# Unit 0's key transfers and row maxima issued from ScalarE's queue, unit 1's input load moved back, and ten constant passes in place of twelve

## The reference

```python
x = x + 0.5 * ffn(layernorm(x), conv_w, conv_b, wqkv, bqkv, wo, bo, ...)   # _L0_ffn_ref
x = x + attn(layernorm(x), Wq, bq, Wk, bk, Wv, bv, Wo, bo)                 # _L0_attn_ref
x = x + 0.5 * ffn(layernorm(x), conv_w, conv_b, wqkv, bqkv, wo, bo, ...)
```

## Time and profile before

| | before |
|---|---|
| median of three executions | 1558.99 us |
| the profiled execution, device time | 1559.22 us |
| its span in the trace | 1557.5 us |
| PE busy | 1502.6 us (96%) |
| DVE, ACT, POOL busy | 1160.8, 1121.3, 1014.9 us |
| chain that ended last, by engine | PE 84%, DVE 8% |
| instructions | 26116 |

### The profile page before, as it was taken

One profiled execution on the slowest core, in us unless ns is written; L12 is line 12 of the kernel. 1 busy time (PEld: TensorE's weight loads), 2 busy tenths in 40 slices (PEclk: granted clock), 3 DMA queues, 4 the chain that ended last, 5 costly groups with the idle time before them and its releaser, 6 DMA issues.

```text
span 1557.5 us, 26116 instructions
## 1 busy us (share of the span) xinstructions
PE 1502.6 (96%) x8318; PEld 832.5 (53%) x8318; DVE 1160.8 (75%) x1834; ACT 1121.3 (72%) x1636; POOL 1014.9 (65%) x978
## 2 busy tenths in 40 slices
PE   4888999999999999999999999999999999999997
PEld 3433555555555555555555555555555555555476
DVE  3767677878778787777877778777777777767486
ACT  2466777677776777777677777777777777777776
POOL 3521668767686776868767686776757677667343
PEclk7799999999999999999999999999999999999999
DMA  7433333152332514233142331514323251521111
GB/s 177 119 92 86 96 87 85 49 140 53 81 91 56 130 42 105 74 88 91 49 131 61 81 92 45 141 48 116 83 75 98 69 117 43 142 51 36 41 43 33
DMA packets 75309, 130.06 MB, mean 84 GB/s; under 512 B 10613, under 2 KB 39206, under 8 KB 70566
## 3 DMA queue, kind: packets, MB, share of 16 engines
q1 hardware_dynamic: 73894, 124.19, 31.2%
q0 software_dynamic: 1280, 4.20, 1.0%
HBM read 97.42 MB, written 29.62 MB: 82 GB/s over the span
## 4 chain that ended last, share of the span: by engine, by line
PE 84%; DVE 8%; issue 3%; SPq 1%; DMA 1%; ACT 1%; POOL 1%; DVEq 0%; ACTq 0%; POOLq 0%
PE hid_y L1013 16%; PE ctx_ps L1208 14%; PE hid_y L1017 13%; PE hid_y L1014 13%; PE score L1056 12%; DVE negmax L881 3%; PE misc L1013 2%; PE score L1076 1%; PE misc L1148 1%; DVE x1n L349 1%; PE score L1013 1%; PE misc L1105 1%; PE misc L1164 1%; PE misc L1141 1%; PE misc L1014 1%
## 5 line engine op out<-in xcount | busy, mean ns | idle before, releaser
L881 DVE TENSOR_REDUCE negmax<-score 128x2 f32<-128x1024 f32 x484 | 590.5, 1220 | 239.4 <-PE score L1056 239.4
L592 POOL TENSOR_TENSOR hidl<-hid,hidh 128x512 fp32r<-128x512 f32 x456 | 584.4, 1293 | 258.1 <-DVE hidh L838 140.8
L711 ACT ACTIVATE probs<-score 128x1024 f32<-128x1024 f32 x468 | 479.5, 1024 | 108.7 <-PE score L1076 108.5
L740 ACT ACTIVATE hid<-hid_y,cols 128x512 f32<-128x512 f32 x484 | 330.9, 684 | 161.9 <-PE hid_y L1017 154.2
L1208 PE MATMUL ctx_ps<-probs,V 128*18 128x512 f32 x2048 | 271.5, 602 | 3.2 <-DVE ctxT L888 3.2
L1056 PE MATMUL score<-Kp,Qp 24*128 24x512 f32 x968 | 244.9, 500 | 23.8 <-DMA Kp<-k_parts_dram 16.1
L1076 PE MATMUL score<-Qp,Kp 32*128 32x512 f32 (+1 forms) x1024 | 265.9, 499 | 0.0
L1013 PE MATMUL hid_y<-x1h,w1h 128*128 128x512 f32 x484 | 236.2, 488 | 1.5 <-DVE negmax L881 1.3
L369 POOL TENSOR_TENSOR yacc<-yacc,gated 128x512 f32<-128x512 f32 x127 | 170.6, 1343 | 61.8 <-DVE gated L854 61.8
L737 ACT ACTIVATE hidh<-hid_y,cols 128x512 fp32r<-128x512 f32 x256 | 174.7, 682 | 34.4 <-PE hid_y L1017 31.9
L1056 PEld LDWEIGHTS score<-Kp,Qp 24*128 24x128 f32 x968 | 90.5, 183 | 197.4 <-issue 138.2
(11 more groups left out here) (203 smaller groups left out, 1828.4 us busy)
## 6 DMA issues: line engine op xcount, KB each, us to landing
gate_b<-gate_dram SPq DMA_DIRECT2D x128, 256.0 KB, 3.6
q_parts_dram<-q_parts SPq DMA_DIRECT2D x48, 256.0 KB, 3.0
k_parts_dram<-k_parts SPq DMA_DIRECT2D x48, 256.0 KB, 3.1
Qp<-q_parts_dram SPq DMA_DIRECT2D x64, 192.0 KB
Kp<-k_parts_dram SPq DMA_DIRECT2D x64, 192.0 KB
Qp<-q_parts_dram SPq DMA_DIRECT2D x30, 240.0 KB
Kp<-k_parts_dram SPq DMA_DIRECT2D x30, 240.0 KB
Qp<-q_parts_dram SPq DMA_DIRECT2D x30, 144.0 KB
```

What stands on the lines that cost most here:

```text
L592: pool.tensor_tensor(hidl[:, n % RING, :], hid[:, n % 2, :], hidh[:, n % RING, :].bitcast(F32), ALU.subtract).then_inc(s["h_lo"], 1)
L711: act.activation(probs[:, n % 2, 2 * j:2 * j + 2, :], score2[:], ACT.Exp, scale=SCALE)\
L740: act.activation(hid[:, n % 2, :], hid_bank(u, n), ACT.Relu, bias=col(n))\
L881: dve.tensor_reduce(negmax[:, g % 2, :, k % 8], banks_for_max(u.count(32, k))[:], AX.X, ALU.max, negate=True).then_inc(s["a_max"], 1)
```

## The change

All of it concerns the first two units.

- k's three writes of unit 0 are issued by ACT's queue, behind ACT's own rounding of k, in place of SP's at T = -22.
- The first chunk of k's packed reads (use 0) is issued by ACT's queue at `FIRST_KEYS_AT` = -5, behind a wait for the three writes, in place of SP's at T = -16. `load_packed` is the old code of the two DMAs, made a function.
- `m_rows` of unit 0 (four DMAs, one per group) is issued by ACT's queue right behind the copy, and SP neither waits for it nor issues it.
- The load of unit 1's rows goes from tick -27, ahead of q's writes, to tick -15, behind the first chunk of q's reads.
- Ten constant passes in place of twelve stand ahead of round 14.

```diff
-CLOCK_FILL = {k: 12 if k == 14 else 1 if k % 2 == 0 else 0 for k in range(14, 56)}
-SECOND_LOAD_AT = -27
+CLOCK_FILL = {k: 10 if k == 14 else 1 if k % 2 == 0 else 0 for k in range(14, 56)}
+MAX_BY_ACT = 1
+SECOND_LOAD_AT = -15
+FIRST_KEYS_AT = -5
...
+        def by_act(n, k):
+
+            return n == 0 and k == 1
+
+        def load_packed(eng, n, k, use, chunk):
+
+            lo, hi = chunks_of(n)[use][chunk]
+            for half, at in enumerate(DATA_AT[use]):
+                eng.dma_start((Qp, Kp)[k][at:at + PRODUCT_ROWS, lo:hi, :].bitcast(F32).rearrange("p i q -> p (i q)"),
+                              dram[k][:, :, PAIRS * half + lo:PAIRS * half + hi, :]
+                              .rearrange("a d i q -> (a d) (i q)")).then_inc(s["pack_in"][use][chunk], 16)
...
-                    if T == at:
+                    if T == at and not by_act(u.n, k):
...
-                if T - 1 in NM_AT:
+                    if (use, chunk) != (0, 0) or not by_act(u.n, k):
+                        wait_sp(s["parts_out"][k], u.count(48, 48))
+                        wait_sp(s[("a_s1", "a_s2")[use]], (u.n - 1) * 32 + TC * chunks_of(u.n)[use][chunk][1])
+                        load_packed(sp, u.n, k, use, chunk)
+
+                if T - 1 in NM_AT and u.n >= MAX_BY_ACT:
...
+                        if by_act(u.n, k):
+                            for part, written in enumerate(("f_p1", "f_p2")):
+                                wait(act, s[written], 2)
+                                for run in RUNS[k][part]:
+                                    act.dma_start(dram[k][run].rearrange("d h q -> h d q"),
+                                                  parts[k][:, part, :].bitcast(F32)).then_inc(s["parts_out"][k], 16)
...
+                if T == FIRST_KEYS_AT and u.n == 0:
+                    act.wait_ge(s["parts_out"][1], 48)
+                    load_packed(act, 0, 1, 0, 0)
...
+                    if u.n < MAX_BY_ACT:
+                        wait(act, s["a_mr"], u.count(4, g + 1))
+                        act.dma_start(Qp[MAX_ROW:MAX_ROW + MAX_ROWS, 2 * g:2 * g + 2, :].bitcast(F32), m_rows[:])\
+                            .then_inc(s["a_m_in"], 16)
```

## The result

The changed kernel takes 1562.97 us (median of 13 executions, 1560.34 to 1567.58), the kernel before 1558.27 us beside it (13 executions, 1555.21 to 1563.26). The ratio is 1.0028, 95% interval 1.0016 to 1.0040: slower by 0.28%, where 1548.0 us was forecast and nothing above 1554.5.

A forecast was written before the change was run, and what follows sets the result against it. PE, busy 96% of the span, was taken as the bound, so early gains stay. Terms -7.0 + 1.0 - 0.3 - 3.9 + 0.6 - 1.7 = -11.3 against 1559.2 gave 1548.0 us, range 1543.5 to 1554.5.

The forecast's parts named there:

- What bounds the kernel: Whole kernel: PE, busy 96% of the span, is one long queue from about 80 us, so early gains stay.
- k's writes on ACT: Front of unit 0: issue 1.82 us, then 4.1 to land; landed at 22.4 instead of 27.9 us.
- k's first read: From k's landing to PE's first round: 6.66 us less 1.7 plus 0.3, so the round starts at 27.7.
- the front: Start up to PE's first round: both moves of k to ACT make it 7.0 us earlier, bounds 2.8 to 10.
- What waits behind it on ACT: ACT's roundings and eviction of V behind k's writes: cost nothing, unless the landing is later than about 26 us.
- Round 8: Second chunks of q and k arrive with no slack left: 1.0 us charged, bounds 0 to 5.
- The reads at 47.61: Reads behind SP's wait for `m_rows` go out some 20 us earlier, behind those PE wants first: 0.
- `m_rows` on ACT: Row maxima writes on ACT's queue: first two groups 0, third -3.9 us (0 to -4.8), fourth +0.6 (0 to +2).
- Rival 2: `m_rows` still waits, its engines busy with the same reads in either queue: -5.7 us, 1553.5, chance 0.14.
- The clock behind that wait: After the third group's wait, shortened to 0.9 us, the clock stays up: -1.7 us (0 to -2).
- Ten passes: Two constant passes fewer before round 14 save 0.7 us, about half given back: -0.3 (0 to -0.7; up to +2).
- The slower rival: ACT is held by its own issues, deciding from about 2 us each: +2.9 us, 1562, chance 0.05.

The follow-up runs named there:

- e6: Kernel before with k's writes and first read on ACT's queue, and the two constant fills issued behind q's writes: 1556.09 us, ratio 0.9986.
- e13: Changed kernel with only the first group of unit 0's maxima back on SP's queue (wait and write): 1557.22 us, ratio 0.9996.
- e12: Kernel before with only unit 1's first read of k moved behind unit 0's third write of maxima: 1554.72 us, ratio 0.9977.
- e9: Kernel before with k's writes and first read on ACT's queue, and unit 0's third write of maxima issued by POOL: 1556.65 us, ratio 0.9983.
- e14: Kernel before with only the fourth group of unit 0's maxima written by ACT, SP still waiting: 1564.99 us, ratio 1.0036.
- e7: Changed kernel with all of unit 0's maxima back on SP's queue and twelve passes in place of ten: 1557.35 us, ratio 0.9992.
- e5: Kernel before with k's writes and first read on ACT's queue, and unit 1's first k read behind the third maxima write: 1552.37 us, ratio 0.9957.
- e4: Kernel before with only unit 0's three k writes and first k read moved to ACT's queue: 1556.67 us, ratio 0.9989.

## Why the prediction was wrong, step by step

**What bounds the kernel.** Right, and with it that a shift of the first 110 us stays to the end: behind 250 us the difference of the two traces moves between 3.5 and 3.8 us only. But 1.5 us of it came on between 126 and 140 us, with the short stretch at the lower clock, where the forecast had nothing behind 110.

**k's writes on ACT.** The direction was right, the size not. Landing at 22.4 was forecast, they landed at about 26.4. The mis-sized term is the issue, 1.82 us; it measured 6.18, since the fills of 13.7 us were in the way (e6: 2.06 us without them). From the end of issue to landing it took 4.0 us, where 4.1 was taken. My upper bound of 3.62 us came from the row that showed this in milder form, and was too low.

**k's first read.** From issue to round 0 it took 4.55 us (26.45 to 31.00, q's first read landing last), where 5.3 was forecast. With both terms the front gained 3.7 of 7.0 us, within its bounds of 2.8 to 10.

**What waits behind it on ACT.** Costed at nothing, with the cover gone if the landing came later than about 26; it came at 26.4. Four weight loads of POOL then ran beside the reads, and the late one of them put ACT's copy of group 1 back by 0.85 us.

**Round 8.** Forecast 1.0 us, measured 0.8 (-3.7 to -2.9). Right, and the working too: its 14.3 us of transfers behind the landing, counted from 26.4 in place of 22.4, give 40.7, and round 8 started at 40.75.

**The reads at 47.61.** This is the step that failed: "go out some 20 us earlier, behind those that PE wants first on the same queue; 0". They went out 15.4 us earlier, but PE did not want them first. It wanted group 1's maxima, which were no longer on that queue and were issued behind them. The wait that I removed from SP was not dead time of a queue; it was what ordered 768 KB behind 16 KB. Price: 7.91 us of wait at round 12, some 5 us of the time (e13), against a forecast gain of 11.3.

**`m_rows` on ACT.** Group 1, charged with 0, is the loss above. Group 3: -3.9 was forecast, the wait went from 4.83 to 3.56 us, and the landing from 6.99 to 6.65. The term that failed is the landing in a queue of its own, 3.2 us. The worth of the wait was right: e12, which holds k's read back, cuts it by 3.9 us. Rival 2 was right in mechanism, and e9 extends it to POOL's queue. Its 1553.5 fell with the step above. Group 4: +0.6 was forecast, and between 0.4 and 1.0 us lies in the trace (PE's lag goes from 1.7 at 96 to 2.7 at 102 and 2.1 at 104 us of before); with SP still held it cost 6.5 us in e14, where the clock fell, which the forecast had not looked at outside the wait at 84.

**The clock behind that wait.** -1.7 was forecast for a short wait. The wait stayed, and the clock fell again, at 86.6, and for longer. Where the wait was short, in e12, it did not fall, and 1.6 us were gained.

**Ten passes.** -0.3 forecast; the ten took 2.83 us, as the clock rose in their midst (59.3); PE had by then been busy since round 12 at 53.98, with one gap of 0.29 us. Nothing to be told in e7.

**The sum.** It gives 1547.9, not 1548.0, which changes nothing.

**The slower rival** had the right sign by the wrong mechanism: ACT's `m_rows` issues cost 0.64 to 0.76 us in the changed kernel, not 2. That the change takes a hold away from transfers that nobody wants yet was among no rivals.

**A faster version.** e5 takes 1552.37 us, 6.5 under the 1558.88 of before beside it (ratio 0.9957), and beats both kernels. It keeps the keys on ACT's queue (worth 1.6 us, e4) and the hold, and issues unit 1's first read of k behind the third write of maxima (worth 4.2 us alone, e12).

## What to carry to other kernels

Before a wait is taken out of a DMA queue, list every transfer behind it and ask whom each will now stand in front of: here a wait that looked idle kept 768 KB behind the 16 KB that PE needed. A small urgent transfer is made fast by what is issued before it, not by the queue that it is in; hold the large reads back until it is out. And look at what a kept wait lets go at the same moment: here a write on ACT's queue and a load on SP's, 0.2 us apart, came with a small gap on PE (0.2 to 0.7 us) and with a fall of the clock that cost some 6 us; which of them leads to which is open.

## What the runs showed that was not expected

- On three queues (SP's, ACT's, POOL's) a 16 KB write stood behind large reads alike: 6.99, 6.65 and 6.5 us to land, and its first packet started 4.1 us (SP's queue), 4.8 and 6.7 us (ACT's) after the issue, where it is 1.3 to 1.5 with no read ahead.
- Fills in pieces of 2 KB that read from few partitions (0.3 us each in the packet records, against 0.08 for other pieces of 2 KB) slowed the next issues on SP's and ACT's queues from 0.6 to some 2 us each in the mean.
- The granted clock can stay at 1.2 GHz with PE's row full: in one execution of e5 for 47.8 us from 80.2 on (that one took 1564.93 us, the other nine 1551.31 to 1555.62). A stretch of it:

```profile
100.00:110.00 10.00, 10.00 (x39) 3.60 (x38) 5.62 (x5) 5.01 (x10) 0.00 (x0) 0.50 0.00 0
```
